# Attention masks on GpSimd: one behind each normalisation of probabilities, in place of a block of three

## The reference, cut to what matters

```python
xn = ln(x, g_norm)
q, k, v = ...                                   # 16 heads of 64; one k, v head, one null key
q = l2norm(q) * q_scale;  k = l2norm(k) * k_scale
sim = einsum('bhid,bjd->bhij', q, k) * 8.0
sim = sim + attn_bias                           # [heads, 128, 129], relative positions, the same for all batches
sim = where(causal, neg, sim); sim = where(mask, sim, neg)
attn = softmax(sim, axis=-1)
y = ln(einsum('bhij,bjd->bhid', attn, v) @ Wout, g_out)
out = x + shared(y) + routed(y)                 # top 2 of 7 experts
```

## Time and profile before

| | before |
|---|---|
| median of 3 runs | 446.83 us (446.19 to 448.18) |
| profiled execution | 446.81 us, of which 445.0 us are the span of instructions |
| busy: TensorE, VectorE, ScalarE, GpSimd | 343.8, 324.1, 274.8, 229.9 us |
| attention steps | about 45 to 293 us of the span |
| a steady step | 12.76 us |
| GpSimd `norm_p`, `add_mask` | 64 of each, mean 1047 and 1191 ns |

### The profile page before, as it was taken

How to read it: one execution, slowest core, us unless ns; L and a number is a source line. 1 busy time by engine, 2 the same in 40 slices (tenths; PEclk the granted TensorE clock), 3 DMA queues, 4 the chain that set the end, 5 groups by cost and what they waited for, 6 DMA issues and landing times.

```text
span 445.0 us, 10196 instructions
## 1 busy us (share of the span) xinstructions
PE 343.8 (77%) x2921; PEld 294.5 (66%) x2922; DVE 324.1 (73%) x1160; ACT 274.8 (62%) x919; POOL 229.9 (52%) x255
## 2 busy tenths in 40 slices
PE   0286754888888998888889687668818999999990
PEld 0285643676776776767767466467808999999980
DVE  1839396799999999999999996658603555555545
ACT  1374673988889888888898476236403444444540
POOL 5025815567677776666677344067760344444430
PEclk9996995999999999999999899569976999999996
DMA  6726299970000000000000000011111212122117
GB/s 180 210 65 195 77 213 203 200 117 0 2 2 1 2 1 3 1 2 1 2 1 3 1 2 1 0 42 49 55 48 41 58 54 64 49 58 58 38 39 246
DMA packets 39479, 26.55 MB, mean 60 GB/s; under 512 B 4464, under 2 KB 37130, under 8 KB 39438
## 3 DMA queue, kind: packets, MB, share of 16 engines
q1 hardware_dynamic: 34256, 20.60, 20.9%
q0 software_dynamic: 2240, 4.23, 2.8%
q10 hardware_dynamic: 2942, 1.21, 1.2%
HBM read 12.89 MB, written 13.54 MB: 59 GB/s over the span
## 4 chain that ended last, share of the span: by engine, by line
PE 39%; DVE 37%; issue 7%; POOL 7%; DMA 4%; ACT 3%; SPq 0%; DVEq 0%; ACTq 0%; POOLq 0%
PE bank L1198 31%; PE bank L1195 8%; POOL sent_rows L539 7%; DVE p_space L1015 6%; DVE norm_in L817 5%; DVE rn L815 4%; DVE low L1019 3%; DVE norm_in L818 2%; DVE rn L819 2%; DVE oT_space L1027 2%; DMA q_space<-in_L_cond_g_dram 1%; DMA bias<-result_rows 1%; DVE norm_in L813 1%; DVE biasm_space L1150 1%; DVE xn L935 1%
## 5 line engine op out<-in xcount | busy, mean ns | idle before, releaser
L689 ACT ACTIVATE p_space<-p_space,low 128x129 f32<-128x129 f32 x256 | 99.4, 396 | 22.9 <-DVE low L1019 22.9
L504 POOL TENSOR_TENSOR p_space<-p_space,inv 128x516 f32<-128x516 f32 x64 | 67.0, 1047 | 84.8 <-DVE inv L1035 84.8
L495 POOL TENSOR_TENSOR biasm_space<-bias,madd 128x516 f32<-128x516 f32 x64 | 74.7, 1191 | 0.1
L1015 DVE SCALAR_TENSOR_TENSOR p_space<-bank,rn,biasm_space 128x129 f32<-128x129 f32 x256 | 71.3, 341 | 4.4 <-PE bank L1198 4.1
L545 POOL DMA_INDIRECT result_rows<-oT_space,dest_ring x38 | 37.6, 990 | 61.2 <-DVE dest_ring L1164 61.2
L769 ACT ACTIVATE biasm_space<-bank 128x384 f32<-128x384 f32 x54 | 26.5, 490 | 58.2 <-PE bank L1195 58.1
L689 ACT ACTIVATION_READ_ACCUMULATOR p_space<-p_space,low 128x1 f32 x256 | 49.4, 193 | 0.0
L1198 PE MATMUL bank<-wo_sb,oT_space 128*128 128x128 f32 x256 | 34.0, 288 | 19.6 <-DVE rn L819 18.8
L1198 PE MATMUL bank<-DT,biasm_space 128*128 (+1 forms) x324 | 45.9, 278 | 1.2 <-ACT biasm_space L769 1.2
L1198 PEld LDWEIGHTS bank<-wo_sb,oT_space 128*128 128x128 f32 x256 | 31.4, 200 | 22.5 <-issue 22.5
L1019 DVE TENSOR_REDUCE low<-p_space 128x4 f32<-128x516 f32 x64 | 44.2, 691 | 2.2
(11 more groups left out here) (220 smaller groups left out, 740.6 us busy)
## 6 DMA issues: line engine op xcount, KB each, us to landing
sent_rows<-fill_row SPq DMA_DIRECT2D x2, 1950.0 KB, 23.8
sent_rows<-fill_row SPq DMA_DIRECT2D x2, 1885.0 KB, 19.4
q_space<-sent_rows SPq DMA_DIRECT2D x38, 65.0 KB
xs<-in_x_dram SPq DMA_DIRECT2D x4, 256.0 KB, 6.4
bias<-bias_rows SPq DMA_DIRECT2D x1, 1024.0 KB, 6.0
xn<-result_rows SPq DMA_DIRECT2D x4, 256.0 KB, 4.5
bias<-result_rows SPq DMA_DIRECT2D x4, 256.0 KB, 5.7
out_dram<-xs SPq DMA_DIRECT2D x4, 256.0 KB, 2.5
```

The source lines that it names most:

```text
L495: nc.gpsimd.tensor_tensor(biasm[:, b % 2, heads, :], bias[:, heads, :], madd[:, b:b + 1, :].to_broadcast([P, HC, KEYS]), ALU.add).then_inc ...
L504: nc.gpsimd.tensor_tensor(v, v, spread(inv[:, b % 2, heads], KEYS), ALU.mult).then_inc(p_normed, 1)
L689: last = nc.scalar.activation(v, v, ACT.Exp, bias=low[:, b % 2, h:h + 1], accum_out=den[:, b % 2, h:h + 1])
L1015: last = nc.vector.scalar_tensor_tensor(Pb[:, q, h, :], src, rn[:, q, h:h + 1], biasm[:, q, h, :], ALU.mult, ALU.add)
```

## The change

In each step GpSimd used to run `add_mask` for chunk 0 between the two normalisations of batch t-2, and then three in a row (chunk 3 of batch t-1, chunks 2 and 1 of batch t). Now one `add_mask` stands behind each of the four normalisations, and all four are for batch t-1. The number of instructions is the same, and no wait is written differently. The masks of chunks 0, 1 and 2 are made one step later than before.

```diff
                 norm_p(2, 3)
+                add_mask(0, 1)
                 norm_p(3, 3)
+                add_mask(1, 1)
                 norm_p(0, 2)
-                add_mask(0, 0)
+                add_mask(2, 1)
                 norm_p(1, 2)
                 add_mask(3, 1)
-                add_mask(2, 0)
-                add_mask(1, 0)
                 if t == 4:
```

## The result

The changed kernel takes **421.31 us** (median of 4, 420.62 to 421.98) against 447.23 of the kernel before (median of 4, 446.19 to 448.18): a ratio of 0.942, 95% interval 0.939 to 0.945. The forecast was 425.7, so the direction and most of the size were right, and the gain was 25.9 us where 21.1 had been worked out. The profiled execution took 421.12 us with a span of 419.3, against 446.81 and 445.0.

The account below looks back on a forecast made before the run. VectorE looked like the bound, with TensorE waiting for its chain each step. Steady steps 18.8 + first steps 2.8 - end 0.5 = 21.1 us, so 446.8 - 21.1 = 425.7 us; range 422.5 to 434.

Parts of the forecast that it names:

- The mechanism: VectorE's chain: L815 and L817 wait for GpSimd's masks beside them; a free chain is 1.87 us shorter.
- TensorE's stays at 11.33 and becomes the bound; only its wait can be saved: Steady steps: from 12.76 to 11.33 us, with each of 13 waits of TensorE gone, 18.8 us in all.
- The loops that were to forbid less: Steady step: other loops stay under TensorE's 11.33 us: VectorE 11.1, projection through chain 10.88, GpSimd 11.1, ScalarE 11.29.
- The 0.2 us given to L813: Start of the steady chain: L813 meets the last 0.2 us of a mask, counted into VectorE's step of 11.1.
- fits by 0.04: Steady step: ScalarE, busy for 11.29 us, fits into 11.33 by 0.04, the narrowest place.
- The first steps: First two chains: L818 of the first freed for 0.94 us, L818 and L819 in step 1 for 1.86; 2.8 together.
- a rival for TensorE's clock: Steps 1 and 2: if TensorE's clock is back sooner, up to 2 us more saved; chance 0.05 with no `root_y` loss.
- The end: Start of `root_y`: a mask holds L813, losing 0.95 us; VectorE comes 0.45 ahead, so -0.5 us net.
- the forecast's 11.9: `keep_y`: by the skill's rule L1040 loses up to 0.8 us, VectorE's step is 11.9, and 7.4 us of gain go.
- VectorE's new wait: Sign of being right: VectorE newly waits for scores or exponentials, 0.2 to 0.5 us a step.
- None of the four: Rivals: part of the gain (0.15, 430 to 435.1), nothing changes (0.04, 446.8), slower (0.03, 456.7), more (0.05, 422.7).
- More than forecast: Rival, chance 0.05: clock back sooner in steps 1 and 2, up to 2 us, and no loss at `root_y`; 422.7 us.

Follow-up runs that it names:

- e1: The changed kernel with its masks still a batch ahead but in their old places, three in a row behind the second normalisation: 446.35 us, ratio 1.002.
- e3: The changed kernel with three masks in a row behind the normalisation of chunk 2, away from VectorE's chain: 423.94 us, ratio 0.951.
- e11: The kernel before with each mask addition replaced by a memset of the same block, which only writes: 420.26 us.
- e15: The kernel before, unchanged, profiled a fourth time to see when its first chain begins: 446.48 us.
- e16: The changed kernel, unaltered, profiled a fourth time to see when its first chain begins: 425.25 us.
- e7: The changed kernel without the projection's last matmul, the null value's part, in each step: 421.26 us, ratio 0.944.
- e6: The changed kernel with two instead of three rounds of the reciprocal square root in the chain of queries' norms: 420.42 us, ratio 0.944.
- e4: The changed kernel with GpSimd's list of the kernel before kept through step 3: 429.09 us, ratio 0.962.

## Why the prediction was right, and where it failed

- **The mechanism was right.** VectorE's chain stood still beside GpSimd's masks and is free now; e1 and e3 show that the place does it, e11 that GpSimd's reading does. No wait named GpSimd, since the held instructions count as busy.
- **The step that failed** is the sentence "TensorE's stays at 11.33 and becomes the bound; only its wait can be saved". TensorE did become the bound, but 11.33 was not its work. The busy time of a step with a wait holds 0.24 us that pipelined matmuls hide when no wait stands between them. Twelve waits were worth 12.79 - 11.10 = 1.69 us each instead of 1.45 and the first one 1.5, 21.8 in all instead of 18.8: 3.0 us of the miss. With this alone put right the sum is 422.7, just inside the stated range of 422.5 to 434; what carried the time out of it is the sooner start, which is chance. Chance also hides the error: e15 and e16 are 21.2 us apart, almost the forecast's 21.1, with steps that differ by 1.69 all the same.
- **The loops that were to forbid less.** None of them sets the step, and the sums of 11.1 for VectorE and GpSimd were a little too high: every second step of e7 takes 10.87. The 0.2 us given to L813 are not there (0.17 us long, free). GpSimd's four pairs take 8.66 and its wait 2.42. ScalarE's "fits by 0.04" was no room of a step either: its busy time is 10.93 in the shorter step, for the same instructions as 11.29 before. Why is not shown; its instructions too overlap where no wait stands between them (an exponential of 0.41 us is followed after 0.30).
- **The first steps**: 2.8 forecast, 3.0 measured. The chain of step 1 gave 1.86 exactly; that of step 0 gave 0.59 instead of 0.94, since its L813 was held for 0.61 us (0.27 before). Up to 2 us were left to a rival for TensorE's clock; its sooner return gave 0.6.
- **The end**: L813 of `root_y` took 1.11 us, as forecast. The scores behind it came 0.69 us late, against 0.5. The reason was the forecast's, the size a little more.
- **`keep_y`** cost nothing: L1040, which reads PSUM, takes 280 to 292 ns over all 16 runs, L925 0.15 to 0.17 us, with masks beside them. The Trainium skill's rule that copies and `tensor_scalar` can take the shared ports (same page and section as above) holds, by that page, only when the operands meet conditions; the forecast's 11.9 left them out. Instructions with one tensor in SBUF are held here all the same, L930 and `scale_y`, though not in a steady step.
- **VectorE's new wait** of 0.2 to 0.5 us a step was not seen; it appeared only in e6, where the chain is shorter still.
- **The rivals.** None of the four happened. "More than forecast" named the right side and nearly the right time (422.7), but its price was the clock and a `root_y` that isn't held, and neither was the main cause.
- **What is left.** 3.0 (steps) + 0.2 (first steps) - 0.2 (`root_y`) is 3.0 of the 4.6 us by which the first pair of spans beat the sum (25.7 - 21.1). 1.7 more is the start, which scatters, and 0.1 is lost behind projection 15.

## What to carry to other kernels

Where two engines read SBUF side by side, look for small VectorE instructions that last exactly until a GpSimd instruction ends; then move GpSimd's work to a stretch whose VectorE instructions the trace shows unheld (here those that read PSUM, and L925 and L1035), and look at what stands beside its new place: one input from SBUF is no safeguard, as L930 and `scale_y` show. The floor of an engine that waits is not its busy time: read it from a place where the same two instructions follow each other without a wait (here 0.89 us against a shown 1.06). And compare kernels over a stretch that doesn't scatter: here one between two landmarks held to 0.3 us, while the spans of one kernel moved by up to 4.8.

## What the runs showed that was not expected

- The start of both kernels has two lengths, 1.6 us apart, by how long eight matmuls at 28 us (1.18 or 1.92 us) and the transposes at 42 us take.
- After TensorE's pauses at `root_y` the granted clock is 0.63 and 0.52 over 226 to 228 and 228 to 230 us in the changed kernel, though TensorE had worked without a pause until 222.7. In e4 it stayed at 0.50 from 233 to 243, and the step took 17.5 us instead of 15.0.
